# A new front for a convolution, attention and experts kernel, and its taps for two images at once

## The chip, the cores and the metric

The kernel runs on one NeuronCore of a Trainium2 chip. Its five engines work on their own and meet at semaphores: TensorE (PE: products and transposes, into the banks of PSUM), VectorE (DVE), ScalarE (ACT), GpSimd (POOL) and SyncE (SP), which issues DMAs. Each engine takes its instructions in order; an instruction that waits holds up everything behind it on that engine. The metric is the device time of one execution in microseconds (us).

## The reference

The input x has 32 images of 16x16 positions with 64 channels, all in fp32. Three layers follow one another:

- `x = x + conv(gn(x))`. `gn` normalizes each image by groups of two channels (32 groups). `conv` forms q, k and v for 8 heads of 32 channels; attention works inside 8x8 windows (four to an image), a 3x3 convolution of v (`w_local`, nine taps) with a bias is added, and an output product leads back to 64 channels.
- `t = t + axial(ln(t))`: attention over the 32 images with scores tied over the 256 positions, a sigmoid gate, an output product.
- `t = t + moe(ln(t))`: a router picks two of 8 experts for each of the 8192 tokens; an expert is `w2(silu(w1 x) * (w3 x))` with 682 hidden units.

## The kernel before, in words

The work is written out by hand as a row of blocks. In each, every engine has its own list, and a block ends when all engines have ended. Weights of the convolution are folded: one 64x64 matrix per head for the scores (`score_w`), one for values with the output product (`value_w`), and nine tap matrices (`tap_w`) that are `w_v`, `w_local` and `w_out` multiplied together. `tap_w` keeps an upper and a lower part in fp32r, a reduced fp32 that TensorE takes in one pass.

1. `constants` (L75): GpSimd makes the identity and the matrix `mean_of_group`.
2. `conv_weights` (L97): SyncE loads all weights and then x; the heads' products (L161, L162); nine taps (L172), copied by VectorE (L207); `weff`, 18 products (L179); the split of `tap_w` by ScalarE (L201) and VectorE (L215).
3. `group_norm` (L218): positions lie on partitions, images and channels beside each other. TensorE sums over positions with `mean_of_group` (L303) for x and, after centering (L339) and squaring (L322), once more; then square root (L325), reciprocal (L347), a Newton step and the scaling (L350). Beside it the experts' weights are loaded (L265 to L269), turned by TensorE (L287, L292) and copied by ScalarE (L316, L318).
4. `conv_attention` (L361): the loop over images. An image is first staged by a DMA (L419), turned by TensorE (L479), copied into window order by ScalarE (`xw`, L575) and into a padded image by GpSimd (`xp`, L450, L455). TensorE's order for image n is: scores of n (L496, L501), values of n (L509), probabilities of n-1 turned (L517), taps of n-1 (L526), right side of n+1 (L488), turning of n+2 (L479), output of n-1 (L541) onto the bank of the taps. VectorE's order is: maximum (L641) and shift (L646) of the first four heads, copy of the values (L634), maximum and shift of the other four, sum (L651) and inverse (L655), copy of the right side of n+1 (L629), the second sum and inverse. ScalarE does the exponents (L595) and copies; GpSimd divides (L461). The residual x and the axial weights are loaded behind the last staging (L430, L719).
5. `axial_weights`, `axial_scores` (L730 to L985), and `dispatch_and_experts` (L1023). Tokens are sent to slots of 512 rows per expert; 39 slot tiles are worked off. For a tile, six chunks of 114 hidden units run through TensorE (L1351), ScalarE (L1458), VectorE (L1750) and TensorE (L1361); the result is turned (L1369), summed and scaled (L1700, L1702), and GpSimd scatters it with four indirect DMAs (L1242) to `chosen_out`. The last seven tiles are narrower (448 down to 64 rows): `depth(k)` makes them 112 to 16 partitions deep, still with four scatters each. When all scatters have landed, SyncE loads both halves (L1193), VectorE adds them (L1768, L1770), and the output is stored.

The lines that make one wait for another around the changed parts are these:

```
eng.wait_ge(staged_n[par], 16 * (pair + 1))   # TensorE, turning of an image
wait(eng, evict_n, n)                         # TensorE, taps of image n: bank free
eng.wait_ge(oc_n, k + 1)                      # GpSimd, scatter of tile k
all_added(eng)                                # SyncE, before the final loads
```

## Time and profile before

| | us |
|---|---|
| median of three runs (961.80 to 964.34) | 963.86 |
| the profiled execution | 959.29 |
| its span, first to last instruction | 957.50 |
| TensorE busy | 827.7 |
| VectorE busy | 622.3 |
| ScalarE busy | 456.7 |
| GpSimd busy | 409.4 |

The profile comes from one execution. Busy time counts instructions on an engine; an engine that waits at a semaphore is idle. Products are pipelined, so a row's time on PE can be longer than the distance to the next row, and the distance is what counts. "PEclk" is the clock granted to TensorE, 1.00 for 2.4 GHz and 0.50 for 1.2 GHz.

### The profile page before, as it was taken

Reading aid. Unit: us, or ns where it says so; the run is one execution under the profiler, and the core shown is the slowest. Engines: PE = TensorE matmul, PEld = TensorE weight load, DVE = VectorE, ACT = ScalarE, POOL = GpSimd, SP = SyncE. Lnnn points to the kernel's source line nnn. Section 1 sums busy time; section 2 is a strip of 40 time slices with the busy share of each in tenths; the row PEclk is TensorE's granted clock in tenths of the full one; section 3 lists DMA queues with packets and bytes.
Section 4 is the critical chain, followed back from the end, with each engine's and each line's share of the span. In section 5 each row is a group of like instructions: output and inputs, shape, how many; then the busy total and the mean of one; then the engine's idle time right before and its main releaser. Section 6 shows DMA issues by size and latency. Waiting matters only on the chain.

```text
span 957.5 us, 24022 instructions
## 1 busy us (share of the span) xinstructions
PE 827.7 (86%) x8420; PEld 502.8 (53%) x8420; DVE 622.3 (65%) x1425; ACT 456.7 (48%) x894; POOL 409.4 (43%) x524
## 2 busy tenths in 40 slices
PE   4777899999999689969989868688979999999940
PEld 4546677777777556637778733222323333333430
DVE  0443787878788457744887865678647667666644
ACT  2042566666666434434545434444535555555520
POOL 0000455555555211100345556666666774444570
PEclk9975999999999789989998989989989999999985
DMA  7212000000006398000000041142142233222108
GB/s 197 58 53 75 14 8 11 8 11 8 11 8 109 126 339 268 3 2 2 14 19 19 21 72 27 34 69 47 32 68 53 50 60 48 40 47 34 20 3 263
DMA packets 156254, 56.29 MB, mean 59 GB/s; under 512 B 121103, under 2 KB 150617, under 8 KB 156176
## 3 DMA queue, kind: packets, MB, share of 16 engines
q1 hardware_dynamic: 142736, 45.69, 21.3%
q0 software_dynamic: 9088, 8.55, 2.7%
q10 hardware_dynamic: 4352, 1.05, 0.5%
q8 instruction: 45, 0.74, 0.3%
q14 instruction: 33, 0.27, 0.1%
HBM read 25.09 MB, written 28.51 MB: 56 GB/s over the span
## 4 chain that ended last, share of the span: by engine, by line
PE 30%; DMA 7%; POOL 6%; DVE 5%; issue 5%; ACT 1%; SPq 1%; ACTq 0%; POOLq 0%; DVEq 0%
PE bank L1351 17%; PE bank L1361 9%; DMA slot_x<-rows,slots 6%; POOL slot_x L1232 4%; PE bank L1369 2%; POOL chosen_out L1242 2%; DVE norm_T L1750 1%; ACT norm_T L1458 1%; DMA ex_gate_id<-slot_x 1%; PE bank L1291 1%; DVE residual L1770 1%; PE bank L1264 1%; SPq L1184 1%; DVE norm_T L1768 1%; DMA norm_T<-chosen_out 1%
## 5 line engine op out<-in xcount | busy, mean ns | idle before, releaser
L1351 PE MATMUL bank<-ex_xt,ex_w 64*114 64x512 f32 (+7 forms) x936 | 217.7, 589 | 28.1 <-DVE ex_xt L1695 13.8
L1750 DVE TENSOR_TENSOR norm_T<-norm_T,bank 114x512 f32<-114x512 f32 (+7 forms) x234 | 142.1, 630 | 101.4 <-ACT norm_T L1458 99.1
L1242 POOL DMA_INDIRECT chosen_out<-ex_out,ex_id x156 | 152.8, 979 | 119.0 <-DVE norm_T L1750 38.6
L1458 ACT ACTIVATE norm_T<-bank 114x512 f32<-114x512 f32 (+7 forms) x234 | 129.9, 558 | 95.6 <-PE bank L1351 94.5
L1232 POOL DMA_INDIRECT slot_x<-rows,slots x128 | 124.3, 971 | 110.4 <-issue 63.6
L1351 PEld LDWEIGHTS bank<-ex_xt,ex_w 64*114 64x114 f32 x936 | 76.8, 179 | 144.4 <-issue 109.0
L461 POOL TENSOR_TENSOR probs<-shifted,win_rden 128x512 f32<-128x512 f32 x64 | 66.7, 1043 | 104.6 <-DVE win_rden L655 98.0
L1361 PE MATMUL bank<-norm_T,ex_w 114*64 114x512 f32 (+7 forms) x468 | 100.2, 563 | 0.3 <-ACT ex_w L1445 0.3
L641 DVE TENSOR_REDUCE win_max<-ps_s 128x8 f32<-128x512 f32 x64 | 44.0, 687 | 36.7 <-PE ps_s L501 36.7
L1361 PEld LDWEIGHTS bank<-norm_T,ex_w 114*64 114x64 f32 x468 | 29.7, 136 | 67.1 <-issue 50.5
L1451 ACT ACTIVATE norm_T<-bank 128x512 f32<-128x512 f32 (+7 forms) x39 | 21.8, 559 | 78.2 <-PE bank L1361 78.2
L646 DVE TENSOR_TENSOR shifted<-ps_s,win_max 128x512 f32<-128x512 f32 x64 | 44.3, 692 | 4.7
L526 PE MATMUL ps_c<-xp,tap_w 128*128 128x256 f32 x288 | 45.5, 304 | 0.0
L595 ACT ACTIVATE shifted<-shifted 128x512 f32<-128x512 f32 x64 | 40.3, 630 | 11.0 <-DVE shifted L646 9.8
L651 DVE TENSOR_REDUCE win_den<-shifted 128x8 f32<-128x512 f32 x64 | 43.2, 675 | 0.3 <-ACT shifted L595 0.3
L586 ACT ACTIVATE values<-ps_yv 128x512 f32<-128x512 f32 x32 | 19.1, 598 | 45.8 <-PE ps_yv L509 45.8
L1291 PEld LDWEIGHTS bank<-wo_sb,av_og 128*128 128x128 f32 x256 | 30.8, 197 | 18.3 <-DVE av_og L1500 11.5
L844 POOL TENSOR_TENSOR residual<-residual,bo_sb 128x512 f32<-128x512 f32 x8 | 10.1, 1265 | 68.5 <-DVE ax_xc L948 68.5
L937 DVE COPY ax_y<-ax_ps_y 128x512 f32<-128x512 f32 x32 | 22.1, 692 | 25.9 <-PE ax_ps_y L871 25.6
L526 PEld LDWEIGHTS ps_c<-xp,tap_w 128*128 128x128 f32 x288 | 38.9, 191 | 0.0
L1291 PE MATMUL bank<-wo_sb,av_og 128*128 128x64 f32 x256 | 33.1, 284 | 6.5 <-DVE av_og L1500 6.5
L488 PE MATMUL ps_yv<-xw,score_w 64*128 64x256 f32 x256 | 37.2, 410 | 1.7 <-DVE values L634 1.2
(259 smaller groups left out, 1465.3 us busy)
## 6 DMA issues: line engine op xcount, KB each, us to landing
slot_x<-blank SPq DMA_DIRECT2D x1, 17028.0 KB, 56.4
ex_x<-slot_x SPq DMA_DIRECT2D x128, 64.0 KB
norm_T<-chosen_out SPq DMA_DIRECT2D x8, 512.0 KB, 7.0
w_in<-in_L_ffn_w_dram SPq DMA_DIRECT2D x24, 168.0 KB
chosen_out<-ex_out,ex_id POOLq DMA_INDIRECT x156, 2.2
wlocal_in<-in_L_conv_w_local_dram SPq DMA_DIRECT2D x2, 1152.0 KB, 7.2
norm_T<-in_x_dram SPq DMA_DIRECT2D x4, 512.0 KB, 8.8
staged<-norm_T SPq DMA_DIRECT2D x32, 64.0 KB, 1.8
```

Source lines behind the costliest of these rows:

```text
L461: eng.tensor_tensor(probs[e][:, :, :], shifted[e][:, :, :], rden[e][:, :].unsqueeze(2).to_broadcast([P, HEADS, WTOK]), ALU.mult).then_inc( ...
L526: last = eng.matmul(ps_c[:, 0:L].rearrange("p (r c) -> p r c", r=SIDE), s.tap_w[:, tap].rearrange("p k c -> p (k c)"), xp[par][:, u:u + SI ...
L641: eng.tensor_reduce(mx[e][:, :], scores(e), AX.X, ALU.max).then_inc(max_n, 1)
L646: eng.tensor_tensor(shifted[e][:, :, :], scores(e), mx[e][:, :].unsqueeze(2).to_broadcast([P, HEADS, WTOK]), ALU.subtract).then_inc(sub_n, 1)
L651: eng.tensor_reduce(den[e][:, :], shifted[e][:, :, :], AX.X, ALU.add).then_inc(den_n, 1)
L1232: eng.indirect_dma_start(s.slot_x[:, :], bass.IndirectOffsetOnAxis(slot[:, k, tile:tile + 1], 0), rows[m % RING][:, k, t, :], None).then_i ...
L1242: eng.indirect_dma_start(s.chosen_out[:, :], bass.IndirectOffsetOnAxis(ex_id[k % OUTS][0:depth(k), j:j + 1].bitcast(U32), 0), out[k % OUTS ...
L1291: last = eng.matmul(ps_r[:, t * C:(t + 1) * C], og[g % 2][:, m, t * P:(t + 1) * P], s.wo[:, m, :], start=(m == 0), stop=(m == 1))
L1351: eng.matmul(ps[b][0:HCHUNK, 0:width(k)], w13[par][halves(i), c * HCHUNK:(c + 1) * HCHUNK], xt[par][halves(i), 0:width(k)], start=True, st ...
L1361: last = eng.matmul(ps_y[halves(i), 0:width(k)], w2[par][:, c, :], h[par][:, c, 0:width(k)], start=(pair == 0), stop=(pair == PAIRS_OF_CHU ...
L1458: eng.activation(act[c % DEEP][:, 0:width(k)], ps_1[c % DEEP][0:HCHUNK, 0:width(k)], ACT.Silu).then_inc(act_n, 1)
L1750: eng.tensor_tensor(h[par][:, c, 0:width(k)], act[c % DEEP][:, 0:width(k)], ps_3[c % deep3(k)][0:HCHUNK, 0:width(k)], ALU.mult).then_inc(h ...
```

## The change

The diff has six parts:

- `constants`, `conv_weights` and `group_norm` become one block, `prologue`. SyncE loads x first, now with image and quarter of an image on the partitions (32 x 4) and 64 positions by 64 channels in each; the weights of the heads are loaded by ScalarE's queue.
- GroupNorm: VectorE takes statistics with 64 `bn_stats` (two halves, 32 groups); the parts of an image are joined by two small products with `part_mean`; the inverse root is made on VectorE by a bit shift and three Newton steps. 12 groups are normalized by ScalarE, 20 by VectorE, each written twice (`twofold`), so that channels come to lie on both halves of the partitions after turning.
- All images are turned in the prologue: eight steps of eight transposes, copied out by ScalarE and VectorE in turn, into window order in `norm_T`. The loop over images has no staging, turning or `xw`; scores, values and right side read `norm_T`.
- The nine taps run for a pair of images, 512 columns each, in the odd image's turn; `xp` holds two images, and there are two tap banks.
- The experts' weights are loaded in the loop over images as rows in blocks of 32 and turned by VectorE's 32x32 transposes, sixteen in all, one behind every odd image. Hidden units are in five chunks of 128 and one of 96 (682 and zeros).
- The narrow tiles keep 128 rows to a block, with as many blocks as needed (`blocks(k)`), and so 4, 3, 3, 2, 2, 1, 1 scatters.

```diff
-def constants(nc, s, sem):
-def conv_weights(nc, ctx, s, a, sem):
+def prologue(nc, ctx, s, a, sem):
...
             @block.sync
             def _(eng):
+                src = a["x"].rearrange("b (q r) c e -> (b q) (r c) e", q=QUARTER)
+                for h in range(2):
+                    some = slice(h * LHALF, (h + 1) * LHALF)
+                    eng.dma_start(x[:, some, :], src[:, some, :]).then_inc(x_in[h], 16)
...
+                def turn(step):
+                    if step == 0:
+                        eng.wait_ge(norm_a, BY_ACT)
+                        eng.wait_ge(norm_d, GROUPS_OF_CHANNELS - BY_ACT)
+                        eng.wait_ge(heads_kept, 2 * HEADS)
+                    if step >= 2:
+                        eng.wait_ge(out_a if step % 2 == 0 else out_d, step // 2)
+                    r, half = divmod(step, 2)
+                    for c in range(WIN):
+                        l = r * SIDE + half * WIN + c
+                        last = eng.transpose(psA[:, step % 2 * 2 + c // 4, c % 4 * P:(c % 4 + 1) * P], twofold[:, l * P:(l + 1) * P], s.ident[:, :])
+                    last.then_inc(turned_n, 1)
...
+                eng.matmul(psG[:, 0:GROUPS_OF_CHANNELS], part_mean[:, :], total[:, :], start=True, stop=True).then_inc(mean_n, 1)
+                tap(0)
+                eng.wait_ge(spread_n, 1)
+                eng.matmul(psG[:, GROUPS_OF_CHANNELS:2 * GROUPS_OF_CHANNELS], part_mean[:, :], var[:, :], start=True, stop=True).then_inc(var_n, 1)
+                for t in range(1, 7):
+                    tap(t)
+                turn(0)
+                turn(1)
+                tap(7)
+                turn(2)
+                turn(3)
+                tap(8)
+                for step in range(4, STEPS):
+                    turn(step)
                 eng.wait_ge(tap_free, TAPS)
...
+                keep_tap(0)
+                keep_tap(1)
+                eng.wait_ge(rstd_n, 1)
+                normalize(0, 2)
+                for t in range(2, 7):
+                    normalize(2 * t - 2, 2 * t)
+                    keep_tap(t)
+                turn_out(0)
+                keep_tap(7)
+                turn_out(2)
+                keep_tap(8)
+                turn_out(4)
+                turn_out(6)
...
+                for h in range(2):
+                    eng.wait_ge(x_in[h], 16)
+                    for g in range(GROUPS_OF_CHANNELS):
+                        mine.did(eng.bn_stats(stats[:, h, g, :], x[:, h * LHALF:(h + 1) * LHALF, 2 * g:2 * g + 2]))
+                mine.settle()
...
+                for g in range(BY_ACT, GROUPS_OF_CHANNELS):
+                    eng.tensor_scalar(both_of_group(g), of_group(g), mean[:, g:g + 1], rstd[:, g:g + 1], ALU.subtract, ALU.mult).then_inc(norm_d, 1)
+                for step in range(1, STEPS, 2):
+                    turn_out(step)
...
-def group_norm(nc, s, a, sem):
...
 def conv_attention(nc, s, a, sem):
+                def load_rows(e):
+                    i = e % 2
+                    wait(eng, rows_turned, 2 * (e - 1))
+                    whole = HID // B32 * B32
+                    for m, name in enumerate(("w1", "w3")):
+                        w = a[f"L1_ffn_{name}"][e]
+                        for lane in range(2):
+                            every, rest = bands(2 * m + lane)
+                            columns = slice(lane * B32, (lane + 1) * B32)
+                            eng.dma_start(w13_rows[i][every, 0:ROW_BLOCKS - 1, :], w[0:whole, columns].rearrange("(b h) c -> h b c", h=B32)).then_inc(rows_in[i], 16)
+                            eng.dma_start(w13_rows[i][rest, ROW_BLOCKS - 1, :], w[whole:HID, columns]).then_inc(rows_in[i], 16)
...
+                eng.wait_ge(rows_zero, 4)
+                load_rows(0)
+                load_rows(1)
                 x = a["x"].rearrange("b (h4 r) c e -> b (h4 r c) e", r=1).rearrange("b (g q) e -> q b g e", q=4)
                 for q in range(4):
                     eng.dma_start(s.x1[q * BATCH:(q + 1) * BATCH, :, :], x[q]).then_inc(s.x1_in, 16)
                 axial_loads(eng, s, a)
+                for e in range(2, EXPERTS):
+                    load_rows(e)
...
-                def convolution(n, par):
-                    eng.wait_ge(xp_n, 2 * n + 2)
-                    wait(eng, evict_n, n)
+                def convolution(pair):
+                    eng.wait_ge(xp_n, 2 * pair + 2)
+                    wait(eng, evict_n, 2 * pair - 2)
                     for tap in range(TAPS):
                         u, w = divmod(tap, 3)
-                        last = eng.matmul(ps_c[:, 0:L].rearrange("p (r c) -> p r c", r=SIDE),
+                        last = eng.matmul(ps_c[pair % 2][:, :].rearrange("p (i r c) -> p i r c", i=2, r=SIDE),
                                           s.tap_w[:, tap].rearrange("p k c -> p (k c)"),
-                                          xp[par][:, u:u + SIDE, w:w + SIDE], start=(tap == 0), stop=False, skip_group_check=True)
+                                          xp[pair % 2][:, :, u:u + SIDE, w:w + SIDE], start=(tap == 0), stop=False, skip_group_check=True)
...
                     if there(n - 1):
                         turn_probs(n - 1, 0)
                         turn_probs(n - 1, 1)
-                        convolution(n - 1, 1 - par)
+                        if n % 2 == 1:
+                            convolution(n // 2)
                     if there(n + 1):
-                        right_side(n + 1, 1 - par)
-                    if there(n + 2):
-                        turn(n + 2, par, pair + 1)
+                        right_side(n + 1)
...
+                def turn_rows(k):
+                    e, second = divmod(k, 2)
+                    i = e % 2
+                    if second == 0:
+                        eng.wait_ge(rows_in[i], 16 * ROW_LOADS * (e // 2 + 1))
+                        eng.transpose(s.w13[:, e, :], w13_rows[i][:, :, :].rearrange("p b c -> p (b c)")).then_inc(rows_turned, 1)
+                    else:
+                        eng.transpose(s.w2[:, e, :, :].rearrange("p k c -> p (k c)"),
+                                      w2_rows[i][:, :, :, :].rearrange("p k l c -> p (k l c)")).then_inc(rows_turned, 1)
...
                         inverse(n, 1)
+                    if there(n) and n % 2 == 1:
+                        turn_rows(n // 2)
...
-HCHUNK, HCHUNKS = 114, 6
-HPAD = HCHUNK * HCHUNKS
+HCHUNK, HCHUNKS = 128, 6
+REST = 96
+HPAD = (HCHUNKS - 1) * HCHUNK + REST
...
+        def blocks(k):
+
+            return -(-width(k) // P)
...
                     eng.wait_ge(oc_n, k + 1)
-                    for j in range(R):
+                    for j in range(blocks(k)):
```

## Rows read from the trace of the kernel before

**Rows 1.** Windows: length, busy (count) of PE, PEld, DVE, ACT, POOL, PEclk, DMA, GB/s

```profile
34.40:89.28 54.88, 42.52 (x272) 28.51 (x272) 26.14 (x18) 16.53 (x27) 0.43 (x4) 0.69 0.28 77
...
89.28:321.20 231.92, 223.35 (x3168) 175.82 (x3168) 176.45 (x320) 147.94 (x289) 117.35 (x195) 0.98 0.10 20
```

**Rows 2.** Windows of 2 us in the front, same columns

```profile
12.00:14.00 2.00, 0.71 (x16) 0.52 (x11) 0.00 (x0) 1.15 (x7) 0.00 (x0) 1.00 1.09 348
...
48.00:50.00 2.00, 0.00 (x0) 0.00 (x0) 0.54 (x1) 1.42 (x1) 0.00 (x0) 0.50 0.41 96
```

**Rows 3.** Timeline of the front: start, duration, engine, line, operation

```profile
3.03 0.60 SPq L134 DMA_DIRECT2D wq_in<-in_L_conv_w_q_dram  x1
...
8.34 9.65 SPq L147 DMA_DIRECT2D norm_T<-in_x_dram  x4
...
27.23 4.23 PE L179 MATMUL psB_w<-wout_in,tapT 128*128 128x64 f32 x36 [0.52 <-DVE tapT L207]
...
33.45 0.76 DVE L215 TENSOR_TENSOR tap_w<-tap,tap_w 128x576 fp32r<-128x576 f32 x1 [0.75 <-ACT tap_w L201]
```

**Rows 4.** Groups by shape: count | busy us, mean ns | idle before

```profile
L1545 DVE TENSOR_TENSOR rt_below_top<-bank,rt_top 128x64 f32<-128x64 f32 x8 | 1.8, 225 | 0.3
...
L347 DVE RECIPROCAL gn_rstd<-gn_fix 128x1024 f32<-128x1024 f32 x1 | 6.6, 6553 | 1.1 <-ACT gn_fix L325 1.1
...
L903 ACT ACTIVATE norm_T<-ax_ps_x,beta_sb,gamma_sb 128x512 f32<-128x512 f32 x16 | 12.5, 779 | 20.7 <-PE ax_ps_x L861 20.7
...
L601 ACT ACTIVATE conv_out<-ps_c,conv_bias 128x256 f32 x28 | 20.0, 713 | 13.6 <-PE ps_c L541 13.6
...
L1695 DVE STREAM_TRANSPOSE ex_xt<-ex_x 128x512 f32<-128x512 f32 x32 | 22.5, 705 | 14.9 <-DMA ex_gate_id<-slot_x 14.9
```

**Rows 5.** Timeline in the experts, VectorE

```profile
879.94 0.15 DVE L1689 COPY ex_gate<-ex_gate_id 128x4 f32<-128x4 f32 x1
...
880.00 0.16 DVE L1690 CAST ex_id<-ex_gate_id 128x4 int32<-128x4 f32 x1
```

**Rows 6.** Timeline, first score product of the loop

```profile
93.61 2.08 PE L488 MATMUL ps_yv<-xw,score_w 64*128 64x256 f32 x8 [0.54 <-ACT xw L575]
```

**Rows 7.** Timeline of one image in the loop, TensorE and VectorE

```profile
110.97 0.22 PE L496 MATMUL ps_s<-ident 128*32 128x2 f32 x2
...
117.79 0.22 PE L496 MATMUL ps_s<-ident 128*32 128x2 f32 x2
...
119.11 0.69 DVE L641 TENSOR_REDUCE win_max<-ps_s 128x8 f32<-128x512 f32 x1 [1.06 <-PE ps_s L501]
...
119.83 1.09 PE L517 MATMUL ps_t<-ident,probs 128*128 128x128 f32 x8
...
120.68 1.42 PE L526 MATMUL ps_c<-xp,tap_w 128*128 128x256 f32 x9
...
122.03 1.13 PE L488 MATMUL ps_yv<-xw,score_w 64*128 64x256 f32 x8
...
123.10 0.66 PE L479 MATMUL ps_x<-ident,staged 128*64 128x128 f32 x8
...
123.32 0.69 DVE L629 COPY score_side<-ps_yv 128x512 f32<-128x512 f32 x1
...
123.59 1.10 PE L541 MATMUL ps_c<-probsT,values 128*64 128x64 f32 x32
```

**Rows 8.** Timeline, DMAs issued by SyncE

```profile
289.68 6.98 SPq L430 DMA_DIRECT2D residual<-in_x_dram  x4
...
880.95 2.08 SPq L1184 DMA_DIRECT2D ex_x<-slot_x  x4
```

**Rows 9.** Timeline of the tail: last results and last scatter

```profile
918.97 0.42 DVE L1702 TENSOR_TENSOR ex_out<-ex_both_halves,ex_gate 48x256 f32<-48x256 f32 x1
...
923.90 0.41 DVE L1702 TENSOR_TENSOR ex_out<-ex_both_halves,ex_gate 16x256 f32<-16x256 f32 x1
...
934.14 0.84 POOL L1242 DMA_INDIRECT chosen_out<-ex_out,ex_id  x1 [0.30 <-issue]
```

More of the change, by code:

```diff
@@ L331, in _ @@
                 mine = Steps(eng, dve_did)
-                for q in range(PARTS):
-                    eng.wait_ge(sums, q + 1)
-                    mine.did(eng.tensor_reduce(mean[:, q * per:(q + 1) * per, :],
-                                               ps[:, q, :].rearrange("p (b g e) -> p b g e", g=groups, e=2), AX.X, ALU.add))
-                eng.wait_ge(sums, PARTS)
-                mine.settle()
-                for h in range(2):
-                    eng.tensor_tensor(half(x, h), half(x, h), spread(mean), ALU.subtract).then_inc(centered, 1)
@@ L340, in _ @@
-                for q in range(PARTS):
-                    eng.wait_ge(sums, PARTS + q + 1)
-                    mine.did(eng.tensor_reduce(var[:, q * per:(q + 1) * per, :],
-                                               ps[:, q, :].rearrange("p (b g e) -> p b g e", g=groups, e=2), AX.X, ALU.add))
-                mine.settle()
-                eng.tensor_scalar(var[:, :, :], var[:, :, :], 1e-5, None, ALU.add).then_inc(var_ready, 1)
-                eng.wait_ge(roots, 1)
-                mine.then(eng.reciprocal(rstd[:, :, :], fix[:, :, :]))
@@ L1155, in all_added @@
             for i, landed in enumerate(added):
[L1156 removed]
+                eng.wait_ge(landed, 16 * sum(blocks(k) for k in range(i, FTILES, len(added))))
         def store(eng, q, j):
```

504 lines of the change are left out of this document (221 added, 283 removed).

## The prediction, before the result was known

> **What bounds the kernel now.** I read the trace by stages first, then each stage by its own wait. The windows [rows 1] split the 957.5 us span. Up to 89.28 us stands the front: weights of the convolution, GroupNorm, turning of the experts' weights. From 89.28 to 321.20 us stands the loop over 32 images. Then come the axial scores, the dispatch and the experts, and a last stretch of scatters, loads, sums and stores. In the second part of the front no engine is the bound: TensorE is 42.5 of 54.9 us busy at a mean granted clock of 0.69, VectorE 26.1. It is a chain, in which one engine works while the others wait. In the loop TensorE is busy 223 of 232 us at clock 0.98: that stage is TensorE's, or of a loop of dependencies close behind it. The timeline of one image [rows 7] shows which. The tail is read from the last results of the experts against the last scatter [rows 9]: the results end at 924.31 us, the scatters start until 934.14, so GpSimd's queue alone holds the end up there.
>
> The profiled execution took 959.29 us (span 957.5 and 1.8 around it); the median of the three timed runs is 963.86, 0.5% more. I work out the difference on the profiled execution and take it off the median.
>
> **The front, part by part.** Before, the first load goes out at 3.03 us, behind the block of constants, and the images' loads are issued from 8.34 to 17.99, behind all weights [rows 3]. After, both halves of the images go first, at about 0.9 us. With 1.05 MB each and the 348 GB/s that the DMA engines reach at 12 to 14 us [rows 2], that is 3.0 us each, with some 2.2 us of issue and landing: 6.2 and 9.3 us. The local weights follow (2.36 MB, 6.8 us) and are in by 17 us, beside VectorE's work.
>
> VectorE then runs 64 bn_stats of 64 elements a partition. No row shows bn_stats. A waited operation on 64 elements takes 0.225 us; two small ones with no wait between them start 0.06 us apart although each lasts 0.15 [rows 4, 5], which with 64 elements at about 1 ns each (the 128x512 transpose takes 0.705 us) is 0.13 us. From the other side, the slowest kind of operation, the reciprocal, takes 6.4 ns an element [rows 4], which would be 0.41 us and more. I take 0.17 us, nearer to the lower rows because nothing stands between these instructions: 10.9 us, to 17.1 us (bounds 8.3 and 26). The Trainium skill (VectorE: DVE Perf Modes, The DRAIN you can't avoid) says that the next operation does not start until the pipe has emptied, semaphore or not. By it the 64 would take 64 x 0.22 = 14.1 us and the total would be 3 us more; the pair of rows above, 0.06 us apart, does not agree, so the sum goes by the rows.
>
> Behind them is a chain of some 25 small operations with waits and two round trips over TensorE: 13 on 32 elements at 0.2 us, six on 64 to 128 elements at 0.25 to 0.3, and two trips of 0.6, estimates from the same rows: 6 us, to 23.1. This takes the place of 32 matmuls of 512 columns, the square over 4096 elements, the reciprocal of 6.55 us and the four passes over all data.
>
> The normalization is 12 ScalarE and 20 VectorE operations of 256 elements, in runs of two channels 256 bytes apart. For ScalarE the nearest rows are the eviction with bias that writes single elements 128 bytes apart (256 elements, 0.713 us) and the one with scale and bias, 512 contiguous elements in 0.779 [rows 4]. Half of the second is 0.39; I take 0.5 start to start. The Trainium skill (SBUF — State Buffer, the note on SBUF cachelines) says that every access to a new 16-byte line costs extra, and that two hits in a line hide it. The eviction with single elements agrees with the first half; by the second, runs of two cost nothing extra, and if they did, 12 x 0.2 = 2.4 us would be added. ScalarE also copies five tap products (0.36 each, by the same rows): 7.8 us, to 31 us. VectorE's 20 x 0.28 = 5.6 lie beside it.
>
> Turning: 64 transposes of 128x128; eight take 0.85 us in the loop [rows 7], so a step is 0.85 us at 2.4 GHz and 1.7 at 1.2. Each step's 1024 elements are copied out in some 1.05 (ScalarE) or 1.25 us (VectorE), estimates from the 512-element rows. With two banks, two steps cost 2.1 us, and the two tap products and copies between them 1 us: 9.2 us. The clock is the question: before, with TensorE idle, it was granted 0.50 at 48 to 50 us [rows 2], so I add 1.5 us: to 41.7 us. Last comes what now ends the weights, unhidden in both kernels: 36 products in 4.2 us from 27.23, then bias, copy and subtraction until 34.21 [rows 3], and the block change: 7.3 us. The front ends at 49.0 instead of 89.28: **-40.3 us**. The experts' weights leave this stage altogether.
>
> **The loop over images.** (a) The first score product starts at 93.61 us [rows 6], 4.3 us behind the block, for the staging load, the turning and the copy. After, it needs none: -3.9. It ran at half clock (2.08 us against 1.13 later, [rows 6, 7]); I count half of that and of the next products: -0.9.
>
> (b) A period. Now it is 6.82 us from one image's scores to the next [rows 7], TensorE without a gap: 2.89 us from scores to the taps, taps 1.35, right side 1.07, turning 0.49, output 1.07. The turning goes. Taps for a pair are 9 products of 512 columns. Now they start 0.150 us apart with 256 columns; the fp32 transposes stream 128 columns in 0.106 us, two cycles a column at 2.4 GHz; at one cycle a column 256 would be 0.107. So 512 is 0.22 if the rest is weight loading that now hides, and 0.30 if nothing does. I take 0.228, 2.05 us for a pair. TensorE's work per pair is then 2 x 5.03 + 2.05 = 12.1 instead of 13.64. But the even image, with no taps, is not TensorE's any more: from the start of VectorE's maximum (119.11) to the end of its copy of the next right side (123.32 + 0.69) are 4.90 us, from a start of scores to the maximum 1.32 [rows 7], with 0.1 to start: 6.32. In the odd image the taps push the right side to 2.89 + 2.05 + 1.07 = 6.01, so TensorE's own 7.08 holds. The transposes of expert rows come behind the odd image's last inverse. A 128x512 one is 0.705 us [rows 4], so 0.9 for 704 and 0.57 for 384: the former delays the next maximum by some 0.13 every fourth image. A pair is 6.32 + 7.08 + 0.07 = 13.47 against 13.64: -0.17 x 16 = -2.7. Most of what TensorE is spared comes back as its wait for VectorE.
>
> (c) The last image's taps now stand before its last turning: -1.3. (d) The row loads: 20 DMAs an expert, mostly runs of 128 bytes. SyncE issued four such of 512 runs in 2.08 us [rows 8]; I take 7.6 us an expert. GpSimd must first zero the buffers (until 6.4 us into the stage), so expert 0 lands at 16.5, and VectorE asks at about 18. No stall; 2 to 5 us if late. The copies into the padded image are GpSimd's, idle half of the stage. Together **-8.8 us**.
>
> **The tail.** The seven last tiles now have 4, 3, 3, 2, 2, 1, 1 scatters instead of four each: 12 fewer. The last of them takes 0.84 us with 0.30 of issue ahead of it [rows 9], so scatters that are ready follow one another every 1.15 us, and I take 0.75 from a result to its first scatter. A tile with two scatters has its result at 919.39 [rows 9], so they start at about 920.1 and 921.3, and the queue is empty before the last two tiles, with one each. The last result ends at 924.31, so the last scatter starts at 925.05 instead of 934.14, which is 9.1 us; the smaller reductions of these tiles bring 0.3: **-9.4 us**. Everything behind it follows. Chunks of 128 hidden units change no column count, so the 8.9 us of a full tile stay.
>
> Sum: 40.3 + 8.8 + 9.4 = 58.5, so 900.8 for the profiled execution, and 963.9 - 58.5 = 905 us by the median.
>
> **Rivals.** Strided front: bn_stats at 0.4 us (+14.7), runs of two at 0.7 to 0.8 on ScalarE (+3), the copies behind the turning at double cost (+5), TensorE at half clock throughout (+4): 932. For it: no row shows such runs on VectorE, and the mean clock of the front's second part was 0.69 [rows 1]. Against: one eviction out of line costs less than double. Uneven taps: 0.30 us a product, so 2.7 a pair; a pair is then 14.12, +0.48 x 16 instead of -2.7: 915. For it: the interval is 0.043 above the streaming rate with nothing to name. Fast front: bn_stats 0.13, no clock loss, ScalarE 0.45: 7 to 9 us less, 897.
>
> Slower than before: the row loads pace the loop. VectorE, in order, stops at images 1, 5, 9 and so on for rows_in. If each of an expert's DMAs took 1.75 us, as each of the four residual loads did on SyncE [rows 8], an expert would need 35 us, eight of them 280, and the stage 64 us more than eight times the 27 of four images: 969. It decides from 34.5 us an expert. Against it: those loads had 2048 runs each, here at most 672. That the change does not do what it says has no opening here: the old front's lines are gone.
>
> **How the numbers follow.** My forecast 0.62 (895 to 914 by its own bounds), fast front 0.12, uneven taps 0.10, strided front 0.13, row loads 0.03. The range that leaves out no more than 2 in 10 is 891 to 928: it takes in the fast front, uneven taps and most of the strided one. All cases but the last are faster; 0.3% (2.9 us) is about what a measurement of this kernel tells from no change. Faster 0.97, same 0.01, slower 0.02.
>
> **What would show it.** The loop's first score product at about 49 us (43 to 60). Image periods that alternate, 6.3 and 7.1 us, with TensorE waiting for VectorE's copy in even images. 144 scatters, the last at the first or second microsecond behind the last result. It is wrong if the front ends beyond 65 us, if VectorE waits for rows, or if the periods are even.

## The result, and the profile after

The changed kernel takes 903.92 us (median of four runs, 901.78 to 908.26) against 962.83 (960.84 to 964.34) for the kernel before: a ratio of 0.9395, with a 95% interval of 0.9355 to 0.9436. Forecast were 905 us and a range of 891 to 928. The profiled execution has a span of 902.8 us, 54.7 less than before, where the sum said 58.5; a second profile of the same kernel (last experiment) has 898.7, 58.8 less. So the total came out, but the parts did not come out one by one, and their misses partly cancel. The windows show it. They are cut where TensorE starts the loop, the axial stage, the dispatch and the experts, and where the last result ends; the columns are those of [rows 1]. Here and below, the lines of a listing are picked from a longer view and need not follow one another in it. Before:

```profile
93.61:321.46 227.85, 222.23 (x3160) 175.12 (x3161) 176.46 (x321) 147.51 (x288) 116.63 (x192) 0.99 0.10 20
321.46:426.84 105.38, 88.89 (x1558) 59.50 (x1559) 62.65 (x141) 42.60 (x80) 11.46 (x12) 0.90 0.54 167
426.84:560.46 133.62, 120.89 (x1698) 97.79 (x1698) 97.51 (x353) 60.71 (x139) 52.19 (x72) 0.93 0.08 18
560.46:924.31 363.85, 334.25 (x1574) 124.08 (x1574) 243.57 (x562) 183.30 (x339) 218.62 (x223) 0.97 0.26 45
924.31:957.50 33.19, 0.00 (x0) 0.00 (x0) 10.48 (x17) 0.00 (x0) 7.92 (x10) 0.51 0.64 190
```

After:

```profile
44.65:273.27 228.62, 212.43 (x2768) 152.46 (x2769) 185.47 (x337) 129.61 (x225) 110.66 (x135) 0.97 0.20 31
273.27:383.08 109.81, 93.17 (x1559) 62.90 (x1559) 62.66 (x141) 42.60 (x80) 11.48 (x13) 0.87 0.51 161
383.08:517.31 134.23, 120.02 (x1698) 96.82 (x1699) 97.43 (x353) 62.35 (x140) 52.95 (x75) 0.93 0.08 18
517.31:878.05 360.74, 335.31 (x1562) 127.02 (x1562) 242.36 (x562) 181.42 (x337) 214.63 (x219) 0.97 0.26 45
878.05:902.80 24.75, 0.00 (x0) 0.00 (x0) 10.44 (x17) 0.00 (x0) 1.83 (x2) 0.54 0.85 255
```

| part, us | before | after | second profile | change | forecast |
|---|---|---|---|---|---|
| up to the first score product | 93.61 | 44.65 | 44.22 | -49.0 | -44.2 (front and its staging) |
| loop over images | 227.85 | 228.62 | 227.12 | +0.8 | -4.9 |
| axial stage | 105.38 | 109.81 | 107.16 | +4.4 | 0 |
| dispatch | 133.62 | 134.23 | 133.97 | +0.6 | 0 |
| experts, to the last result | 363.85 | 360.74 | 361.5 | -3.1 | -0.3 |
| last result to the end | 33.19 | 24.75 | 24.7 | -8.4 | -9.1 |

The front is a chain in this order (start, duration, engine, line, operation): statistics, normalization, turning, the tap matrices, and the first score product of the loop.

```profile
6.76 8.17 DVE L295 BATCH_NORM_STATS2 gn_stats<-residual 128x6 f32<-128x64 f32 x64 [5.82 <-DMA residual<-in_x_dram]
21.53 6.55 DVE L318 TENSOR_SCALAR conv_out<-residual,gn_mean,gn_rstd 128x256 f32<-128x256 f32 x20
28.78 1.97 PE L192 MATMUL psA_w<-ident,conv_out 128*128 128x128 f32 x16 [1.01 <-ACT conv_out L245]
38.27 4.13 PE L229 MATMUL psB_w<-wout_in,tapT 128*128 128x64 f32 x36
44.65 2.08 PE L474 MATMUL ps_yv<-norm_T,score_w 64*128 64x256 f32 x8 [1.93 <-PEq L131]
```

In the loop, a pair of images on TensorE, and the two copies, ScalarE's and VectorE's, that the scores at 112.41 us wait for (the lines at 115.61 and 117.42 are the second and the ninth of the nine tap products):

```profile
106.26 0.22 PE L482 MATMUL ps_s<-ident 128*32 128x2 f32 x2
109.73 1.14 PE L474 MATMUL ps_yv<-norm_T,score_w 64*128 64x256 f32 x8 [0.34 <-DVE values L603]
111.48 0.58 ACT L554 ACTIVATE score_side<-ps_yv 128x512 f32<-128x512 f32 x1
111.66 0.65 DVE L598 COPY score_side<-ps_yv 128x512 f32<-128x512 f32 x1
112.41 0.20 PE L482 MATMUL ps_s<-ident 128*32 128x2 f32 x2 [0.46 <-ACT score_side L554]
115.27 2.57 PE L512 MATMUL ps_c<-xp,tap_w 128*128 128x512 f32 x9
115.61 0.43 PE L512 MATMUL ps_c<-xp,tap_w 128*128 128x512 f32 x1
117.42 0.42 PE L512 MATMUL ps_c<-xp,tap_w 128*128 128x512 f32 x1
117.77 1.13 PE L474 MATMUL ps_yv<-norm_T,score_w 64*128 64x256 f32 x8
119.92 0.22 PE L482 MATMUL ps_s<-ident 128*32 128x2 f32 x2
```

From scores to scores the even image takes 6.15 us, in which TensorE waits twice, and the odd one 7.51, in which it does not. Both waits are for VectorE. The first names its copy of the values. The second names ScalarE's half of the copy of the right side, but that half ended at 112.06 us and VectorE's at 112.31, just before the scores. At the end the last scatter now follows the last result ([rows 9] after):

```profile
877.83 0.22 DVE L1698 TENSOR_TENSOR ex_out<-ex_both_halves,ex_gate 128x64 f32<-128x64 f32 x1
879.28 0.91 POOL L1235 DMA_INDIRECT chosen_out<-ex_out,ex_id  x1 [0.30 <-issue]
```

### The profile page after: what moved, and what is told of

It reads as the page before. It is cut to its first block, busy times and chain, and to the rows that moved or that the text cites. A ratio compares the mean times of both kernels' runs of the same rounds, so it can differ in the third digit from the quotient of the medians.

```text
span 902.8 us, 21978 instructions
## 1 busy us (share of the span) xinstructions
PE 787.4 (87%) x7804; PEld 463.7 (51%) x7804; DVE 623.5 (69%) x1522; ACT 434.5 (48%) x828; POOL 394.1 (44%) x452
## 4 chain that ended last, share of the span: by engine, by line
PE 34%; DVE 11%; issue 5%; POOL 3%; DMA 2%; ACT 1%; SPq 1%; ACTq 0%; POOLq 0%; DVEq 0%
PE bank L1346 17%; PE bank L1356 9%; POOL slot_x L1224 2%; PE bank L1284 2%; PE bank L1364 2%; POOL chosen_out L1235 1%; DVE norm_T L1746 1%; DMA slot_x<-rows,slots 1%; PE bank L1275 1%; PE bank L1257 1%; PE bank L1266 1%; PE bank L1293 1%; DVE av_og L1495 1%; ACT norm_T L1453 1%; DVE residual L1766 1%
## 5 line engine op out<-in xcount | busy, mean ns | idle before, releaser
L1346 PE MATMUL bank<-ex_xt,ex_w 64*128 64x512 f32 (+9 forms) x936 | 217.5, 590 | 26.2 <-DVE norm_T L1746 10.6
L1746 DVE TENSOR_TENSOR norm_T<-norm_T,bank 128x512 f32<-128x512 f32 (+7 forms) x234 | 141.9, 629 | 102.1 <-ACT norm_T L1453 99.2
L1235 POOL DMA_INDIRECT chosen_out<-ex_out,ex_id x144 | 142.9, 992 | 119.3 <-DVE norm_T L1746 47.7
L1453 ACT ACTIVATE norm_T<-bank 128x512 f32<-128x512 f32 (+7 forms) x234 | 129.8, 558 | 94.0 <-PE bank L1346 92.7
L1346 PEld LDWEIGHTS bank<-ex_xt,ex_w 64*128 64x128 f32 (+1 forms) x936 | 80.0, 186 | 140.0 <-issue 107.2
L1356 PE MATMUL bank<-norm_T,ex_w 128*64 128x512 f32 (+7 forms) x468 | 102.6, 574 | 0.7 <-ACT ex_w L1440 0.7
L1356 PEld LDWEIGHTS bank<-norm_T,ex_w 128*64 128x64 f32 x468 | 30.3, 139 | 68.6 <-issue 51.5
L1446 ACT ACTIVATE norm_T<-bank 128x512 f32<-128x512 f32 (+7 forms) x39 | 21.8, 559 | 80.5 <-PE bank L1356 80.5
L615 DVE TENSOR_TENSOR shifted<-ps_s,win_max 128x512 f32<-128x512 f32 x64 | 44.2, 691 | 2.2
L474 PE MATMUL ps_yv<-norm_T,score_w 64*128 64x256 f32 x256 | 38.2, 417 | 7.9 <-DVE values L603 6.0
L512 PE MATMUL ps_c<-xp,tap_w 128*128 128x512 f32 x144 | 41.0, 430 | 0.0
L527 PEld LDWEIGHTS ps_c<-probsT,values 128*64 128x64 f32 x1024 | 32.5, 138 | 10.7 <-issue 10.5
```

What stands on the lines that cost most here:

```text
L512: last = eng.matmul(ps_c[pair % 2][:, :].rearrange("p (i r c) -> p i r c", i=2, r=SIDE), s.tap_w[:, tap].rearrange("p k c -> p (k c)"), xp ...
L615: eng.tensor_tensor(shifted[e][:, :, :], scores(e), mx[e][:, :].unsqueeze(2).to_broadcast([P, HEADS, WTOK]), ALU.subtract).then_inc(sub_n, 1)
L1235: eng.indirect_dma_start(s.chosen_out[:, :], bass.IndirectOffsetOnAxis(ex_id[k % OUTS][some, j:j + 1].bitcast(U32), 0), out[k % OUTS][some ...
L1346: eng.matmul(ps[b][0:units(c), 0:width(k)], w13[par][halves(i), c * HCHUNK:c * HCHUNK + units(c)], xt[par][halves(i), 0:width(k)], start=T ...
L1356: last = eng.matmul(ps_y[halves(i), 0:width(k)], w2[par][0:units(c), c, :], h[par][0:units(c), c, 0:width(k)], start=(pair == 0), stop=(pa ...
L1453: eng.activation(act[c % DEEP][0:units(c), 0:width(k)], ps_1[c % DEEP][0:units(c), 0:width(k)], ACT.Silu).then_inc(act_n, 1)
```

## The experiments

All of them start from the changed kernel. Ratios are to the kernel before on the same chip, with 95% intervals.

**Taps per image.** A bank for each of two images; the nine products, of 256 columns again, go back to every turn.

```diff
-                        if n % 2 == 1:
-                            convolution(n // 2)
+                        convolution(n - 1)
...
```

> The changed kernel with the taps run for every image again (nine products of 256 columns in each turn, a bank of its own for each of two images); all else stays. In the changed kernel's profile a pair of images takes 13.65 us (even 6.14, odd 7.53) and the span is 902.8. Theory (pairing piles TensorE's work on the odd image, while the even one falls to a limit of VectorE's): every image now has 2.89 + 1.35 + 1.07 + 1.07 = 6.38 us of TensorE, above the 6.14 of the even image, so a pair takes 12.76, 0.89 less; 16 pairs give -14 us, a span of about 888. Rival 1 (VectorE and the copies hold an image near 6.8 however the taps lie, since a pair took 13.75 before and takes 13.65 now): a pair stays at 13.6, the span within 2 us of 902.8. Rival 2 (pairing saves TensorE 2.70 - 2.49 = 0.2 us a pair and that is all it does): 13.9 a pair, the span 906.

Measured: 888.3 us, ratio 0.9247 (0.9212 to 0.9282), span 886.7. From the third on, every image takes 6.39 us:

```profile
113.89 0.22 PE L482 MATMUL ps_s<-ident 128*32 128x2 f32 x2
116.78 1.42 PE L512 MATMUL ps_c<-xp,tap_w 128*128 128x256 f32 x9
118.13 1.13 PE L474 MATMUL ps_yv<-norm_T,score_w 64*128 64x256 f32 x8
120.28 0.22 PE L482 MATMUL ps_s<-ident 128*32 128x2 f32 x2
```

12.78 a pair where the theory said 12.76; both rivals fall. So this one part of the change made the kernel slower. Without it the kernel is some 14 us faster by the ratios, of which the loop has 12 to 13 (215.3 us against 228.6 and 227.1).

**Taps split over the two turns.** Still 512 columns, four products in the even turn and five in the odd one.

```diff
-                    for tap in range(TAPS):
+                    for tap in (range(4, TAPS) if second else range(4)):
```

> The changed kernel, taps still run for a pair with 512 columns, but four of the nine in the even image's turn and five in the odd one's. Theory (the uneven load of the two images is the loss): even 5.03 + 4 x 0.276 = 6.13 us of TensorE beside VectorE's 6.14, odd 5.03 + 5 x 0.276 = 6.41; a pair takes 12.55 instead of 13.65, 16 of them -17.6 us, a span of about 885. Rival 1 (VectorE's own loop near 6.8): a pair stays at 13.6. Rival 2 (taps ahead of the right side in the even image make VectorE's copy of it late by their 1.1 us, the even image becomes 7.2): a pair of 13.6, no gain either, but with TensorE and VectorE waiting for each other in the even image.

Measured: 888.03 us, ratio 0.925 (0.9222 to 0.9279). The even image takes 6.23 us and the odd one 6.50:

```profile
115.85 1.27 PE L513 MATMUL ps_c<-xp,tap_w 128*128 128x512 f32 x4
117.05 1.13 PE L474 MATMUL ps_yv<-norm_T,score_w 64*128 64x256 f32 x8
122.08 1.53 PE L513 MATMUL ps_c<-xp,tap_w 128*128 128x512 f32 x5
123.54 1.14 PE L474 MATMUL ps_yv<-norm_T,score_w 64*128 64x256 f32 x8
```

The uneven load was the loss: 1.20 us of taps put into the even image lengthen it by 0.08, and the odd one is 1.0 shorter. But the two parts take 1.20 + 1.46 = 2.66 us, where one run of nine takes 2.49 on the mean: a second run of products costs 0.17 us. Per pair, wide taps are then worth 0.04 us over narrow ones (2.70).

**Idle transposes at the loop's start.**

```diff
+                def warm(times):
+                    for w in range(times):
+                        eng.transpose(ps_c[1][:, 0:P], s.ident[:, :], s.ident[:, :])
...
+                    if n == 0:
+                        warm(6)
...
+                    if n == 0:
+                        warm(5)
...
                 right_side(0)
+                warm(5)
```

Eight more stand at the end of the front. In the order of the program it is 8, then 5 behind the first right side, 6 behind the first values and 5 behind the second right side, and not the 6, 5 and 5 that the expectation gives.

> The changed kernel with 24 transposes of the identity that nobody reads, put where TensorE stands idle at the start of the loop over images: 8 at the end of the front, 6 behind the first right side, 5 behind the first values, 5 behind the second right side. In the changed kernel the clock is granted at 0.50 from about 43 to 60.7 us, and from the first score product (44.65) to the scores of image 3 (71.45) pass 26.8 us; before, 24.2. Theory (the half clock is the cost, and TensorE's idling brings it): the clock stays at 1.00 for most of this stretch, the first score product takes 1.13 instead of 2.08, image 1 (10.0 us) takes about 7.5, and the stretch shrinks by 3.5 to 4.5 us. Rival 1 (copies and the waits for them set the start, the clock is beside the point): less than 1 us. Rival 2 (these idle gaps don't bring the clock down, something else does): the clock stays at 0.50 and the stretch gets 1 to 2 us longer by the added products.

Measured: 897.07 us, ratio 0.9334 (0.9306 to 0.9362). This interval just overlaps that of the changed kernel (0.9355 to 0.9436), so the gain is read from the profile. Three windows of 16 us, of the changed kernel, of its second profile (last experiment) and of this one (columns as in [rows 1]; the third last is the granted clock):

```profile
44.65:60.66 16.01, 13.40 (x93) 8.01 (x93) 9.14 (x16) 4.40 (x8) 10.51 (x17) 0.50 0.22 34
44.22:60.23 16.01, 12.67 (x98) 7.92 (x99) 9.75 (x17) 5.12 (x10) 10.51 (x17) 0.70 0.23 34
44.79:60.80 16.01, 14.42 (x163) 10.22 (x167) 11.48 (x21) 6.60 (x12) 11.57 (x18) 1.00 0.21 32
```

The clock stays at 2.4 GHz from the front on. The first product takes 1.14 us, image 0 6.13 instead of 7.67, image 1 7.50 instead of 10.03, and the stretch up to image 3 is 23.5 us instead of 26.8: 3.3 less. Against the second profile, where the clock was back earlier and the stretch took 25.2, it is 1.7. Part of the gain went into a new wait, VectorE's for the first expert's rows:

```profile
62.64 0.91 DVE L643 STREAM_TRANSPOSE w<-w_rows 128x704 f32<-128x704 f32 x1 [1.65 <-DMA w_rows<-in_L_ffn_w_dram]
```

That is the rival of the row loads in small: in the changed kernel, where VectorE asks for these rows at 65.77 us, the slow start hides it.

**Four scatters for every tile.** depth(k) partitions for the narrow tiles, as before.

```diff
-                    for j in range(blocks(k)):
+                    for j in range(R):
...
-                        some = slice(0, rows_of(k, j))
+                        some = slice(0, depth(k))
...
```

> The changed kernel with the narrow tiles as they were before: depth(k) partitions and four scatters for each of the last seven tiles, 156 scatters instead of 144. Theory (the queue of scatters alone held up the end): from the last result to the last scatter 9.8 us as before instead of 1.2, so the span is 8.6 longer, 911.4. Rival (the end came from elsewhere, such as chunks of 128 units in the narrow tiles, or the landing of the scatters behind the last is hidden by what follows): under 3 us.

Measured: 912.68 us, ratio 0.95 (0.9472 to 0.9528), span 911.2.

```profile
877.68 0.41 DVE L1693 TENSOR_TENSOR ex_out<-ex_both_halves,ex_gate 16x256 f32<-16x256 f32 x1
887.83 0.84 POOL L1231 DMA_INDIRECT chosen_out<-ex_out,ex_id  x1 [0.30 <-issue]
```

From the last result to the last scatter 9.7 us as against 1.2, as the theory says. Besides, the experts up to the last result take 364.0 us, as before the change (363.9), where the changed kernel has 360.7 and eight others between 359.6 and 361.5 (one, with the split taps, 362.7): so the 3 us there belong to the narrow tiles as well, and not to the chunks of 128 units, which this run keeps.

**Taps that read in one run.** It leaves out the convolution's shifts.

```diff
...
-                                          xp[pair % 2][:, :, u:u + SIDE, w:w + SIDE], start=(tap == 0), stop=False, skip_group_check=True)
+                                          xp[pair % 2][:, :, :, :].rearrange("p i r c -> p (i r c)")[:, 0:2 * L], start=(tap == 0), stop=False, skip_group_check=True)
```

> The changed kernel with each of a pair's nine tap products reading the first 512 elements of the padded image pair in one run, instead of 32 rows of 16; it leaves out the shifts of the convolution, so only its time counts. In the changed kernel these products start 0.276 us apart, where the prediction took 0.228. Theory (the rows of 16 are what costs: nine products of 256 columns take 1.35 us and of 512 take 2.47, so 0.49 ns a column instead of the 0.42 of one column a cycle at 2.4 GHz): 0.22 to 0.23 us apart, the odd image 0.45 shorter, 16 times 0.45 = 7 us off the loop. Rival 1 (each product carries 0.06 us that has nothing to do with how it reads): 0.276 as now, the loop the same. Rival 2 (the kind of number, fp32r, streams at 0.49 ns a column whatever the rows): also 0.276; this run can't tell it from rival 1.

Measured: one time of 898.23 us, no interval. The odd image takes 7.27 instead of 7.51. The nine products, the second and the ninth of them, and what follows:

```profile
100.44 2.32 PE L512 MATMUL ps_c<-xp,tap_w 128*128 128x512 f32 x9
100.76 0.40 PE L512 MATMUL ps_c<-xp,tap_w 128*128 128x512 f32 x1
102.37 0.40 PE L512 MATMUL ps_c<-xp,tap_w 128*128 128x512 f32 x1
102.69 1.14 PE L474 MATMUL ps_yv<-norm_T,score_w 64*128 64x256 f32 x8
```

The expectation works with means: 2.25 us for nine is 0.250 each, and 2.49 is 0.276. The single starts tell more. From the second to the ninth product are seven distances: 1.61 us here, 0.23 each, and 1.81 in the changed kernel (115.61 to 117.42), 0.26 each. In the kernel before, with 256 columns in rows of 16, they are 0.13 each (the first line is the second and third product, the other the ninth):

```profile
120.89 0.42 PE L526 MATMUL ps_c<-xp,tap_w 128*128 128x256 f32 x2
121.81 0.29 PE L526 MATMUL ps_c<-xp,tap_w 128*128 128x256 f32 x1
```

So contiguous reading gives the 0.22 to 0.23 of the theory, and rows of 16 add 0.03 a product. What is left belongs neither to the product nor to the kind of number, and so both rivals fall: nine distances of 0.13, 0.26 and 0.23 make 1.18, 2.34 and 2.07 us, and the runs take 1.35, 2.49 and 2.25, 0.15 to 0.18 more each time. That is the cost of changing to a run of taps and from it, the same that splitting the run in two cost above. Where in the change it arises, no run here shows.

**x behind the local weights.**

```diff
-                for h in range(2):
-                    some = slice(h * LHALF, (h + 1) * LHALF)
-                    eng.dma_start(x[:, some, :], src[:, some, :]).then_inc(x_in[h], 16)
...
                         eng.dma_start(wlocal[:, k, 3 * i:3 * i + 3, :], local[k][:, 3 * i:3 * i + 3, :]).then_inc(local_in[i], 16)
+                for h in range(2):
+                    some = slice(h * LHALF, (h + 1) * LHALF)
+                    eng.dma_start(x[:, some, :], src[:, some, :]).then_inc(x_in[h], 16)
```

> The changed kernel with the two loads of x issued behind the six loads of the local weights (2.36 MB) instead of ahead of them. In the changed kernel the first bn_stats starts at 6.76 us and the first score product at 44.65. Theory (the front is one chain from x on, and the order of the loads carries part of its gain): bn_stats starts 6.5 to 7 us later, near 13.5, and everything up to the first score product moves with it, to 51; less by the 1 to 2 us in which the tap products no longer stand in the way of the turning. Rival (the weights' side is as long as x's, since the tap products and their copies run until 35 us in the changed kernel): the first score product moves by under 3 us, because the weights come 6 us earlier.

Measured: one time of 909.1 us.

```profile
13.74 8.17 DVE L295 BATCH_NORM_STATS2 gn_stats<-residual 128x6 f32<-128x64 f32 x64 [12.80 <-DMA residual<-in_x_dram]
51.63 2.08 PE L474 MATMUL ps_yv<-norm_T,score_w 64*128 64x256 f32 x8 [1.93 <-PEq L131]
```

The statistics start 6.98 us later, and the first score product too: nothing on the weights' side is near the path, and by this one profile 7 of the 49 us are the order of the loads.

**Taps per image, idle transposes, rows zeroed first.** Beside the first and the third edit above:

```diff
+                    eng.memset(w13_rows[i][:, :, :], 0.0).then_inc(rows_zero, 1)
+                    eng.memset(w2_rows[i][:, :, :, :], 0.0).then_inc(rows_zero, 1)
                 eng.memset(one[:, :], 1.0).then_inc(zero_n, 1)
...
                 padded(1)
-                    eng.memset(w13_rows[i][:, :, :], 0.0).then_inc(rows_zero, 1)
-                    eng.memset(w2_rows[i][:, :, :, :], 0.0).then_inc(rows_zero, 1)
```

> Three edits together on the changed kernel: taps per image (a pair took 12.78 instead of 13.65), the idle transposes at the start of the loop (clock 1.00 from the front on), and GpSimd zeroing the buffers of the experts' rows ahead of everything else in the loop, so that the row loads start about 4 us earlier (with the idle transposes alone VectorE waited 1.65 us for the first rows at 62.6 us). Theory (the three are independent): -14 us by the taps, -3.3 to -6 by the start with the wait for rows gone, so a span of 880 to 884 and a time near 883. Rival 1 (a shorter first image brings VectorE to the first rows so early that it waits again, 2 us or more): 886. Rival 2 (GpSimd's later padded images hold up the taps of image 0 at its start): a wait of TensorE for xp in the second turn, 1 to 2 us.

Measured: 885.86 us, ratio 0.9228 (0.9191 to 0.9266), span 881.2. The first rows are turned at 59.34 us with no wait, images take 6.35 to 6.40 from the second on, and the loop is 211.4 us as against 215.3 with taps per image alone. The times overlap with that kernel's; only the profile tells the two apart.

**The write of empty slots moved into the loop.**

```diff
                     load_rows(e)
+                    if 3 <= e < 7:
+                        some = slice((e - 3) * (BLANK + 1) // 4, (e - 2) * (BLANK + 1) // 4)
+                        eng.dma_start(slots[:, some, :], empty.to_broadcast([P, some.stop - some.start, R * ROW])).then_inc(s.blank_n, 16)
...
-                eng.dma_start(s.slot_x[:, :].rearrange("(k p r) c -> p k (r c)", p=P, r=R),
-                              s.blank[:, :, :].rearrange("p r c -> p (r c)").unsqueeze(1).to_broadcast([P, BLANK + 1, R * ROW])).then_inc(s.blank_n, 16)
...
```

> The changed kernel with the 17 MB write of empty slots (slot_x<-blank), which SyncE issues at the start of the axial scores, cut in four and issued in the loop over images instead, each piece behind the row loads of an expert (numbers 3 to 6). The axial stage, from its first product to the first of the dispatch, took 105.3 us before, and 109.8, 106.4, 108.5, 105.1 and 108.3 in the five profiles since, with one or two idle times of TensorE of up to 2.2 us each that wait for no semaphore, all while the DMA engines are full with this write, and in most of them the clock falls to 0.50 behind one. Theory (TensorE waits for its own instructions, whose loads queue behind that write): without it in this stage these stalls are gone and the stage takes 102 to 104 us; the loop over images gets stalls of the same kind, up to 4 us in all, or none where its idle time covers them. Rival (the stalls belong to the place in the program and not to the write): the stage stays at 105 to 110.

Measured: 897.88 us, ratio 0.9354 (0.9314 to 0.9393). The interval overlaps the changed kernel's, so here too the profile decides. What the write does in the changed kernel's axial stage: the longest of TensorE's idle times without a semaphore ("issue"), and products at half clock behind it (3.67 us for 16, which take 2.00 elsewhere in the stage):

```profile
308.40 0.42 PE L860 MATMUL ax_ps_a<-ax_y,norm_T 64*32 64x128 f32 x6 [2.16 <-issue]
311.47 3.67 PE L834 MATMUL ax_ps_f<-fold,conv_out 128*128 128x64 f32 x16
```

The clock there (third last column) and the DMA engines, busy throughout (second last):

```profile
310.00:312.00 2.00, 2.00 (x7) 0.53 (x3) 1.83 (x7) 0.94 (x2) 0.00 (x0) 0.50 1.10 341
```

The loop and the axial stage with the write moved:

```profile
44.35:271.78 227.43, 210.50 (x2768) 151.75 (x2769) 185.26 (x337) 129.41 (x225) 110.95 (x137) 0.98 0.44 108
271.78:373.60 101.82, 87.92 (x1559) 59.41 (x1559) 62.56 (x141) 42.58 (x80) 11.14 (x11) 0.90 0.01 2
```

The stage takes 101.8 us, less than in any of ten profiles with the write in place (105.1 to 109.8), and no idle time on "issue" above 0.4 us is left in it; the loop got none. So the stalls belong to the write. That it is TensorE's own code that waits is inferred, but from more than the stalls: the profile has 12 packets and 0.20 MB on an instruction queue in this stage, with the write and without it. In the ten profiles with the write there are 21 such idle times, and each ends 1.2 to 1.6 us after one of these packets has landed (in the changed kernel a packet landed at 307.06, and TensorE went on at 308.40). Whose code the queue carries, the trace does not say. The Trainium skill (Runtime: NRT & Kernel Launch, Instruction fetch mechanics) says that code comes in blocks of 16 KiB by a DMA queue of the sequencer's own; 12 packets of 0.20 MB agree with the size. It calls the cost mostly hidden; behind this write, if the inference holds, it was up to 2.2 us, and the clock.

**All four edits, and the changed kernel again.** No new edit: the last two kernels in one, and the changed kernel as it is.

> The changed kernel with taps per image, the idle transposes at the start of the loop, the buffers of the experts' rows zeroed first, and the write of empty slots cut in four and issued in the loop: the last two runs in one kernel. Theory (independent of each other): the loop as in the kernel with the first three edits (211.4 us from the first score product to the axial stage), the axial stage as in the one with the last (101.8 instead of 105.6), so a span of about 877.5 and a time 8.4% below before, ratio about 0.916. Rival (a shorter loop leaves the pieces of the write less room between the row loads, which come late): VectorE waits for rows in one or more odd images, some 2 to 6 us in all, span 880 to 884.

> The changed kernel itself, unaltered, beside the combined one and the kernel before, for a second profile and a ratio on the same chip. Expected: the ratio of before again 0.94 (0.9355 to 0.9436 at first); the span within 3 us of 902.8, where a difference, if it comes, lies in the axial stage (first product to first of the dispatch, 109.8 us in the first profile, 105.1 to 108.5 in the others with that write in place): about 107 there, so a span near 900. If the stage is at 109.8 again, its length belongs to the changed kernel and not to the execution.

Measured on one chip: all four 881.02 us, ratio 0.917 (0.9138 to 0.9203); the changed kernel again 902.03, ratio 0.9403 (0.9367 to 0.9439). Of the combined kernel the loop and the axial stage:

```profile
44.71:256.10 211.39, 207.15 (x2929) 162.12 (x2929) 185.35 (x337) 132.21 (x225) 110.83 (x137) 1.00 0.47 116
256.10:357.98 101.88, 87.97 (x1559) 59.42 (x1559) 62.63 (x141) 42.57 (x80) 11.14 (x10) 0.90 0.01 2
```

Both are as in the separate runs; images stay at 6.39, so the rows are not late. The span is 879.4 and not 877.5, because the dispatch took 136.6 us (132.5 to 136.0 in the other profiles), which stays open. This version beats both kernels: 2.3% faster than the changed one. The changed kernel's second profile has 107.2 in the axial stage, so the 109.8 belonged to the execution and not to the kernel.

## Why the prediction was right

**The front** went as told, in the order told, with two steps longer and four shorter than forecast. x was in at 6.76 us (6.2 forecast). The 64 bn_stats took 8.17, forecast 10.9: each lasts 0.204 but they start 0.126 apart, the lower bound of 0.13 and not the 0.17 taken. The Trainium skill (VectorE: DVE Perf Modes, The DRAIN you can't avoid) says that the next operation does not start until the pipe is empty, and in the same paragraph that one which is not held starts earlier. The prediction took the first sentence alone, which gave 14.1 us; the trace agrees with the second. The small chain took 6.6 (6.0), the normalization 7.2 (7.8). Its operations, where nothing stands between them, start 0.49 us apart on ScalarE (0.5 taken) and 0.32 on VectorE (0.28); what the runs of two channels cost in this stays open, as no run has the same operations on contiguous elements. The turning took 9.5. The forecast had 9.2, though its own parts (4 x 2.1 + 1) add up to 9.4, and 1.5 more for the clock, which was granted at 1.00 throughout. From the last turning to the first score product were 6.4 (7.3). Together the front is 4.8 us better than forecast. As to this stage the rival of the fast front came true rather than the forecast: its terms (bn_stats at 0.13, no clock loss, ScalarE at 0.45) add up to 2.6 + 1.5 + 0.6 = 4.7 us, and not to the 7 to 9 that it was given. The strided front and its 0.4 us per bn_stats are refuted.

**The loop** had the right mechanism and the wrong sizes. That the even image falls to VectorE's limit and TensorE waits there, with periods that alternate, was forecast and is shown by the two runs on the taps. But the sum for a pair, 13.47 against 13.64, failed on both sides. The odd image is 7.51 and not 7.08, because the taps of a pair take 2.49 us and not 2.05. The step that failed there is the interval of 0.150 us: it is the mean over a run that has 0.17 us of its own at its ends, and the products themselves start 0.13 apart. The prediction took the excess for a cost of each product that a wider one would hide; in fact 512 columns in rows of 16 take twice what 256 do (0.26), and joining two runs saves one 0.17, once a pair. The even image was a little better than forecast, 6.15. And the 13.64 took one image of 6.82 us [rows 7] twice, where every other image before took 6.92 (the five parts read from that row add up to 6.87, half of the true pair). A pair went from 13.75 to 13.65. The rival of uneven taps had 0.30 a product, nearer to the mean of 0.276 than the 0.228, and the total not (915).

What failed outright is the step "I count half of that and of the next products: -0.9". The full clock did not come sooner but later. The windows of the changed kernel from the turning on (columns as in [rows 1]):

```profile
36.00:38.00 2.00, 1.76 (x15) 1.51 (x15) 1.22 (x1) 0.82 (x2) 0.00 (x0) 1.00 0.00 0
42.00:44.00 2.00, 0.73 (x8) 0.57 (x7) 0.64 (x2) 0.71 (x2) 0.00 (x0) 0.89 0.00 0
44.00:46.00 2.00, 1.35 (x6) 1.26 (x8) 0.33 (x2) 0.00 (x0) 1.30 (x4) 0.50 0.00 0
60.00:62.00 2.00, 2.00 (x10) 1.69 (x9) 1.93 (x4) 1.88 (x4) 0.00 (x0) 0.84 0.33 52
```

TensorE stood idle from 42.72 to 44.65, the clock fell to 0.50 and in this profile rose only in the first pair's taps, at about 60.6 us; before, it rose in the first image. The start up to image 3 became 2.6 us longer (1.0 in the second profile), and the idle transposes, which give 3.3 (1.7) back, show why. The last images brought 1.0 instead of 1.3.

**The row loads** stalled nobody, but only behind the slow start: with the idle transposes they came 1.65 us too late, so the margin was not the comfortable one that I argued.

**The tail** was right about the queue (8.6 of the 9.1) and missed the narrow tiles' own work: 3.1 us instead of 0.3, which four scatters take back to 364.0.

**The axial stage** was costed at nothing since the diff does not touch it; it moved by 1.8 and 4.4 us in two profiles of the same kernel. A forecast from one execution carries that much on it, and the total within 1.1 us of the median is partly luck: a front 4.8 us better and experts 2.8 better against a loop 5.7 and an axial stage 4.4 worse. The signs that were named all came: the first score product between 43 and 60 us, periods that alternate with TensorE waiting for VectorE, 144 scatters, and the last of them 1.2 us behind the last result.

## What to carry to other kernels

Work saved on the busiest engine counts only up to the next engine's limit in the same turn of the loop: before joining work of two turns into one, write down each turn's load on every engine, since an uneven pair can cost more than the joining saves (here joining spared TensorE 0.2 us a pair, and the pair still took 0.9 more than with the taps apart). What joining saves is found from single starts, not from the mean of a run, which hides what the run costs at its ends. A base period is read from a whole pair or more, not from one row. When a stage is shortened, look at what now starts on an idle or half-clocked engine, and at loads that were hidden by the slow stage.

## What the runs showed of the hardware that was not expected

- A 17 MB write that fills the DMA engines stalls TensorE with no semaphore in play, up to 2.2 us at a time, and each of the 21 stalls ends 1.2 to 1.6 us after an instruction packet has landed; in the changed kernel's profile the clock fell behind one, and products such as those at 311.47 us ran at half clock. With the write in place the stage took from 105.1 to 109.8 us in ten profiles, without it 101.8 and 101.9 in two.
- Unwaited bn_stats of 64 elements start 0.126 us apart though each lasts 0.204.
- Products of 512 fp32r columns that read rows of 16 start 0.26 us apart, contiguous ones 0.23, and those of 256 columns in rows of 16 0.13. A run of four, five or nine of them, between products of other kinds, costs some 0.17 us besides.
- Around 1.9 us of idle TensorE at a change of blocks the clock fell, and over the next 16 us it was 0.50 in one profile of the changed kernel and 0.70 in another; with 24 transposes in the idle times, 1.00 all through.
